# A graph layer on one core: edge products in rows of eight tiles, steps of 34 tiles, gathers without a per-gather wait

## What is computed

```python
h = relu(layernorm(x))
deg = max(segment_sum(1, dst), 1);  w = (deg[src] * deg[dst]) ** -0.5
edge_msg = relu(edge_attr @ W1e + b1e) @ W2e + b2e
agg = segment_sum((h[src] + edge_msg) * w, dst)
combined = (1 + gin_eps) * h + agg
out = h + relu(combined @ W1n + b1n) @ W2n + b2n
out = out * rsqrt(mean(out * out) + RMS_EPS) * rms_w
return x + out
```

## Time and profile before

| | |
|---|---|
| median device time of three runs | 1413.84 us |
| span of the profiled execution, first to last instruction | 1158.9 us |
| mean granted TensorE clock | 0.993 |
| busy TensorE, VectorE, ScalarE, GpSimd | 1061.3, 964.8, 734.5, 809.0 us |
| degree part (one-hot compares done to degrees ready) | 46.0 to 67.6 us |
| edge loop: first look, first products, last sum into the accumulator | 91.2, 103.5, 1106.5 us |
| gathers (L1008) | 784, mean 977 ns |

### The profile page before, as it was taken

The page is one execution under the profiler, slowest core; times in us unless marked ns, Lnnn a source line. Parts: engine busy times, 40 slices in busy tenths (PEclk is TensorE's granted clock), DMA queues, the critical chain, the costliest instruction groups (busy, mean ns, idle before and its releaser), DMA issues. The chain is left out here.

```text
span 1158.9 us, 35277 instructions
## 1 busy us (share of the span) xinstructions
PE 1061.3 (92%) x12293; PEld 764.4 (66%) x12293; DVE 964.8 (83%) x4508; ACT 734.5 (63%) x1317; POOL 809.0 (70%) x826
## 2 busy tenths in 40 slices
PE   0335999999999999999999999999999999999986
PEld 0322677777677777777777777777777777777753
DVE  7799988888888888888888888878888888888468
ACT  6953766666666666666666666666666666666535
POOL 1046777777777777777777777777777777777464
PEclk9999999999999999999999999999999999999988
DMA  6035444444444444444444444444444444443463
GB/s 221 1 142 156 133 118 120 129 118 120 130 119 118 129 120 118 129 120 119 128 120 119 128 119 119 130 118 120 128 118 120 129 118 120 130 119 80 129 255 119
DMA packets 67388, 145.56 MB, mean 126 GB/s; under 512 B 24163, under 2 KB 25750, under 8 KB 66832
## 3 DMA queue, kind: packets, MB, share of 16 engines
q1 hardware_dynamic: 41120, 88.27, 24.5%
q0 software_dynamic: 25088, 51.83, 18.8%
q10 hardware_dynamic: 1008, 3.21, 0.8%
HBM read 136.67 MB, written 6.57 MB: 124 GB/s over the span
## 5 line engine op out<-in xcount | busy, mean ns | idle before, releaser
L1008 POOL DMA_INDIRECT arena<-node_rows,idx x784 | 765.9, 977 | 247.7 <-issue 199.5
L1168 ACT ACTIVATE arena<-bank 128x686 f16<-128x686 f32 x414 | 375.9, 908 | 204.9 <-PE bank L1078 204.0
L1160 ACT ACTIVATE arena<-bank 128x512 f32<-128x512 f32 (+1 forms) x460 | 250.6, 555 | 157.3 <-PE bank L1033 141.0
L1089 PE MATMUL bank<-t_words,arena 128*126 128x256 f16 x2254 | 302.8, 275 | 0.4 <-ACT arena L1168 0.4
L1234 DVE SCALAR_TENSOR_TENSOR arena<-iota_h,hi_f,bank 128x98 f32<-128x98 f32 x828 | 226.1, 309 | 82.3 <-PE bank L1043 82.1
L1033 PE MATMUL bank<-w1e,arena 64*128 64x128 f32 x3312 | 253.9, 273 | 0.0
L1218 DVE TENSOR_SCALAR arena<-iota_c,code 128x343 f16<-128x343 f16 x828 | 241.6, 334 | 6.6 <-PE bank L1078 4.8
L1089 PEld LDWEIGHTS bank<-t_words,arena 128*126 128x126 f16 x2254 | 238.0, 136 | 1.7 <-ACT arena L1168 0.7
L1033 PEld LDWEIGHTS bank<-w1e,arena 64*128 64x128 f32 x3312 | 222.4, 191 | 0.0
L1078 PE MATMUL bank<-arena 128*128 128x343 f16 x828 | 190.6, 312 | 0.2
L1204 DVE TENSOR_SCALAR arena<-arena,part_f 128x256 f16<-128x256 uint8 x414 | 147.1, 355 | 0.8 <-DVE t_words L612 0.6
(11 more groups left out here) (199 smaller groups left out, 863.7 us busy)
## 6 DMA issues: line engine op xcount, KB each, us to landing
arena<-in_attr SPq DMA_DIRECT2D x138, 384.0 KB
arena<-low_src SPq DMA_DIRECT2D x48, 288.0 KB, 5.4
arena<-node_rows,idx POOLq DMA_INDIRECT x784
node_rows<-arena SPq DMA_DIRECT2D x1, 3160.5 KB, 8.9
arena<-in_x ACTq DMA_DIRECT2D x7, 448.0 KB, 10.9
arena<-in_x SPq DMA_DIRECT2D x6, 512.0 KB, 13.4
out<-arena SPq DMA_DIRECT2D x12, 224.0 KB
arena<-node_rows SPq DMA_DIRECT2D x4, 516.0 KB, 8.8
```

Of the source, the lines that this page charges most:

```text
L1008: nc.gpsimd.indirect_dma_start(out=edge_rows[:, u, j, 0:ROW], out_offset=None, in_=table, in_offset=bass.IndirectOffsetOnAxis(ap=idx[:, u, ...
L1089: mm = nc.tensor.matmul(x_sum[0:XC, 0:2 * D], strip[:, u, k, :], T16[:, k, :], start=k == 0, stop=k == NBLK - 1)
L1160: ins = nc.scalar.activation(out.rearrange("p (j o) d -> p o j d", o=2), of, ACT.Relu)
L1168: nc.scalar.activation(strip[:, u, :, 2 * p * W:2 * p * W + 2 * W].rearrange("p k (t w) -> p t k w", t=2), pair_bank[:, :].rearrange("p (t ...
```

## The change

A step takes 34 tiles, 18 dense and 16 gathered, so there are 48 steps; the last 20 hold 33 tiles. A step has five **phases** instead of nine rounds. A phase does the edge products of two units, that is of eight tiles (six in phase 2, four in phase 4), into a product buffer whose full width is used; the looks of four tiles; and two pairs of counts, one right behind the products and one behind the spread. The spread takes 8, 8, 16 and 17 blocks in phases 0 to 3. All four units of gathered sums of the step before stand at the end of phase 1, all five of dense sums at the end of phase 4. Row buffers of VectorE's one-hot matrices go from 3 to 4 (`RL`) and from 2 to 3 (`PB`). The gathers lose their wait per gather and keep the one for the sums. The attribute loads are cut 8, 7 and 2 pairs. The degree part compares half steps of 17 tiles, 96 of them.

```diff
-TD, TG = 18, 18
+TD, TG = 18, 16
 TS = TD + TG
-U = TS // 4
+LOOKS = [0, 2, 4, 6, 8, 9]
 UNITS_D = [(0, 4), (4, 4), (8, 4), (12, 4), (16, 2)]
-UNITS_G = [(0, 2), (2, 4), (6, 4), (10, 4), (14, 4)]
+UNITS_G = [(0, 4), (4, 4), (8, 4), (12, 4)]
 UD, UG = len(UNITS_D), len(UNITS_G)
+U = UD + UG
+PHASES = [(0, 1), (2, 3), (4, 5), (6, 7), (8,)]
+NPH = len(PHASES)
+SPREAD_AT = [0, 8, 16, 32, 49, 49]
 UL = TD // 2
-RL = 3
+RL = 4
+PB = 3
...
+ATTR_PAIRS = [0, 8, 15, 17]
+ATTR_PHASES = [0, 2, 4, 5]
...
+DT = TS // 2
+DC = DT * W
...
-                rel_t = rel.rearrange("p (j t) -> p j t", t=TD)
+                rel_t = rel.rearrange("p (j t) -> p j t", t=DT)
...
                     for j in fetched(c, i):
-                        if c > 0:
-                            pool.wait_ge(strip_ready if j % 2 else z_ps, (c - 1) * U + (j // 2 + 5))
                         nc.gpsimd.indirect_dma_start(
...
+            def edge_mlp(c, u, p):
+
+                if p in ATTR_PHASES:
+                    pe.wait_ge(attr_in[u][ATTR_PHASES.index(p)], (c - u) * 8 + 16)
+                if not (isinstance(c, int) and c * U + PHASES[p][0] < 1):
+                    pe.wait_ge(r_ready, c * U + PHASES[p][0])
+                pairs = pairs_of(p)
                 for odd in range(2):
                     rowsof = slice(odd * ED, odd * ED + ED)
-                    nc.tensor.matmul(z_bank[:, odd * 512:odd * 512 + 2 * D], ones_bf[rowsof, :],
-                                     bias_split[rowsof, 0, 0:2 * D], start=True, stop=False)
-                for j in range(2):
+                    nc.tensor.matmul(z_bank[:, odd * 512:odd * 512 + len(pairs) * D], ones_bf[rowsof, :],
+                                     bias_split[rowsof, 0, 0:len(pairs) * D], start=True, stop=False)
+                for j, pair in enumerate(pairs):
                     for odd in range(2):
                         rowsof = slice(odd * ED, odd * ED + ED)
                         at = odd * 512 + j * D
-                        mm = nc.tensor.matmul(z_bank[:, at:at + D], attr[rowsof, u, 2 * k + j, :], w1e[rowsof, :],
-                                              start=False, stop=j == 1)
+                        mm = nc.tensor.matmul(z_bank[:, at:at + D], attr[rowsof, u, pair, :], w1e[rowsof, :],
+                                              start=False, stop=j == len(pairs) - 1)
                 mm.then_inc(z_ps, 1)

-            def look(c, k):
-
-                pe.wait_ge(low_t_ready, c * UL + (k + 1))
-                if not (isinstance(c, int) and c * UL + k < 1):
-                    pe.wait_ge(s_ready, c * UL + k)
-                for j in range(2):
-                    mm = nc.tensor.matmul(look_ps[:, j * LK:(j + 1) * LK], low_t[:, k % RL, j, :], s_parts[:, :],
-                                          start=True, stop=True)
+            def look(c, p):
...
             def one(c, u):
-                for k in range(U):
+                for p in range(NPH):
+                    counts = range(2 * p, min(2 * p + 2, NA))
                     if live(c):
-                        edge_mlp(c, u, k)
+                        edge_mlp(c, u, p)
+                        count_pair(c, u, counts[0])
                     if live(c + 1):
-                        look(c + 1, k)
-                    if c == S and k == 0:
-                        for b in range(7):
-                            spread_rows(c - 1, 1 - u, b)
-                    elif c < S and live(c - 1) and 1 <= k < 8:
-                        spread_rows(c - 1, 1 - u, k - 1)
-                    if live(c):
-                        count_pair(c, u, k)
-                    if live(c - 2) and k == 2:
+                        look(c + 1, p)
+                    if live(c - 2) and p == 0:
                         window_gathered(c - 2)
                         window_dense(c - 2)
-                    if live(c - 1) and k < UG:
-                        sum_gathered(c - 1, 1 - u, k)
-                    if live(c - 1) and k == 6:
+                    if c == S and p == 0:
+                        spread_rows(c - 1, 1 - u, 0, NBLK)
+                    elif c < S and live(c - 1) and SPREAD_AT[p] < SPREAD_AT[p + 1]:
+                        spread_rows(c - 1, 1 - u, SPREAD_AT[p], SPREAD_AT[p + 1])
+                    if live(c) and len(counts) > 1:
+                        count_pair(c, u, counts[1])
+                    if live(c - 1) and p == 1:
+                        for i in range(UG):
+                            sum_gathered(c - 1, 1 - u, i)
+                    if live(c - 1) and p == NPH - 1:
                         turn(c - 1)
-                    if live(c) and k >= U - 4:
-                        sum_dense(c, k - (U - 4))
-                        if k == U - 1:
-                            sum_dense(c, UD - 1)
+                    if live(c) and p == NPH - 1:
+                        for k in range(UD):
+                            sum_dense(c, k)
             steps(pe, one)
...
             def one(c, u):
+                if live(c - 2):
+                    act.wait_ge(turned_ps, c - 1)
+                    if not (isinstance(c, int) and c < 3):
+                        act.wait_ge(win_d_ps, c - 2)
+                    nc.scalar.activation(turned, turned_bank, ACT.Copy).then_inc(turned_ready, 1)
                 if live(c - 1):
                     act.wait_ge(summed_d, c * UD)
                     if not (isinstance(c, int) and c < 2):
                         act.wait_ge(turned_ps, c - 1)
                     nc.scalar.activation(sum_d, sum_d_ps, ACT.Copy).then_inc(sum_d_ready, 1)
-                for k in range(U):
-                    if live(c - 1) and k == 5:
+                for p in range(NPH):
+                    if live(c - 1) and p == 2:
                         act.wait_ge(summed_g, c * UG)
                         if not (isinstance(c, int) and c < 2):
                             act.wait_ge(win_g_ps, c - 1)
                         nc.scalar.activation(sum_g, sum_g_ps, ACT.Copy).then_inc(sum_g_ready, 1)
-                    if live(c - 1) and k == 7:
-                        act.wait_ge(turned_ps, c)
-                        if not (isinstance(c, int) and c < 2):
-                            act.wait_ge(win_d_ps, c - 1)
-                        nc.scalar.activation(turned, turned_bank, ACT.Copy).then_inc(turned_ready, 1)
                     if live(c):
-                        relu(c, u, k)
-                        if k < NA:
+                        for k in PHASES[p]:
+                            relu(c, u, k)
                             keep_counts(c, u, k)
             steps(act, one)
...
+            def pairs_ahead(c, u, which):
+                if live(c):
+                    pair(c, u, which)
+
             def one(c, u):
+                for p in range(NPH):
+                    last = p == NPH - 1
+                    if c == S + 1 and p == 0:
                         nc.vector.tensor_scalar(rel_s[:, :, :], rel_s[:, :, :], float(-W), None, ALU.add)
                         step(nc.vector.tensor_scalar(rel_d[:, :, :], rel_d[:, :, :], float(-W), None, ALU.add))
+                    if c == -1 and p < 4:
+                        encode(nc, p, code, hi_f, rel_d, loop.scratch, step)
+                    if last:
+                        pairs_ahead(c + 1, 1 - u, 0)
+                    else:
+                        pairs_ahead(c, u, 2 * p + 2)
+                    if live(c + 1) and not last:
+                        for k in range(LOOKS[p + 1], LOOKS[p + 2]):
+                            turn_low(c + 1, 1 - u, k)
+                    if live(c + 2) and last:
+                        for k in range(LOOKS[0], LOOKS[1]):
+                            turn_low(c + 2, u, k)
+                    if live(c - 1) and p == 0:
+                        scale_gathered(c - 1, 1 - u, 2)
+                        scale_gathered(c - 1, 1 - u, 3)
+                    if live(c - 1) and last:
+                        keep_x(c - 1)
+                    if live(c) and p < 3:
+                        for j in range(2 * p, min(2 * p + 2, UD)):
+                            match_dense(c, j)
+                    if live(c - 2) and p == 1:
+                        add_windows(c - 2)
+                    if live(c - 1) and p == 2:
+                        places(c - 1)
+                    if live(c) and p in (2, 3):
+                        for j in (range(0, 3) if p == 2 else range(3, UD)):
+                            scale_dense(c, u, j)
                     if live(c + 1):
+                        for k in range(LOOKS[p], LOOKS[p + 1]):
+                            pick_s(c + 1, 1 - u, k)
+                    if live(c) and p in (2, 3):
+                        match_gathered(c, 2 * p - 4)
+                        match_gathered(c, 2 * p - 3)
+                    if last:
+                        pairs_ahead(c + 1, 1 - u, 1)
+                    elif 2 * p + 3 < NA:
```

(20 more changed lines are left out.)

145 lines of the change are left out of this document (54 added, 91 removed).

## The result

The changed kernel takes 1953.55 us (median of four runs, 1945.93 to 1956.55) against 1413.53 us: ratio 1.381, interval [1.377, 1.384]. The forecast was 1371, range 1356 to 1403. It was wrong by 583 us, and the change made the kernel slower instead of faster.

A forecast was written before the change was run, and what follows sets the result against it. TensorE was taken to set the step, with GpSimd full too. 47 steps of 19.7 us, 5 hold and 1 outside make 931.9 against 974.4, so 1413.84 - 42.5 = 1371 us, range 1356 to 1403.

The forecast's parts named there:

- the span and the median: Whole run: profiled span 1158.9 us, median of runs 1413.84; the 254.9 us between them were carried over unchanged.
- Taking the per-gather wait away saves no time at once, since it costs none: GpSimd's gathers: the 0.30 us before each is no wait, so removing the wait was priced at no saving.
- hold of 5 us: Edge loop: GpSimd's gathers let step 28 start only at about 657 us, where TensorE alone would be at 651.5.
- Rival A: Edge loop: GpSimd becomes the bound beside denser VectorE work, gather pitch 1.275 to 1.33 us; 1401 us, chance 0.18.
- C: Edge loop: TensorE and ScalarE alternate, 0.35 us lost in each of four phases, step 21.1 us; 1432 us, chance 0.08.
- D: TensorE's gaps are semaphore waits, not array changes, so the new order keeps them; step 20.9 us, 1423 us, chance 0.06.
- the 0.6 us of stalls: TensorE waits for ScalarE's copy at phase 1's second count, 0.2 us, and at phase 4's count, 0.4 us, each step.
- Step 19.7: Edge loop: a step falls from 21.65 us to 19.1 by TensorE's work, plus 0.6 of stalls, making 19.7 us.
- GpSimd full: Edge loop of the kernel before: 17 gathers at 1.275 us take 21.68 us, so GpSimd is full in step with TensorE.
- Prelude +1: Before and after the loop: 96 half-step columns instead of 92 cost 0.9 us; net +1, range -1 to +7.
- Compares at 1.02: Degree part: seven compares with rows of 17 bf16 instead of 18 stay at 1.02 us each; cost 0, possibly +6.5.

The follow-up runs named there:

- b1_same: The kernel before, unchanged, run again at the upper level to get a trace: 1438.23 us, beside 1435.44 for the kernel before.
- a2_after: The changed kernel, with nothing further changed, run again at the lower level: 1132.74 us against 1159.58 for the kernel before.

## Why the prediction was wrong

**The step that failed first: the span and the median.** The prediction found 254.9 us between span and median and carried them over. They do not lie there: b1_same has 1.7 us between span and run, the changed kernel's profiled execution 1.7 (1944.2 to 1945.93). They lie in the loop, 5.5 us in each of 46 steps, and the trace shown is of an execution without them. That was the sign to read: the page describes another level than the one that is timed, so the margins in the earlier trace rows could not be trusted for it.

**The step that failed worst: "Taking the per-gather wait away saves no time at once, since it costs none".** With it the sum put the loss by gathers at 0 beyond the hold of 5 us. True at the lower level, where the earlier trace rows were taken. At the upper level that wait was what kept the kernel before at 1435: without it 1784.04, and with such a wait the changed kernel takes 1616.46 instead of 1945.6. The wait is worth 329 to 349 us; the other 182 us of the changed kernel's loss stay open. The prediction asked what the wait costs, and what follows when GpSimd starts later, never what a wait holds back that starts too early. Rival A came nearest in place (GpSimd beside denser work) but had the direction wrong: GpSimd did not get slower (996 ns a gather at the lower level and 964 at the upper, 977 in the kernel before), it held the others up. C and D were about TensorE and ScalarE. (D's 20.9 us a step also leaves out the 0.6 us of stalls that the forecast has; with them it is 21.5.)

**The rest, held against a2_after at the lower level.** Span 1131.0 against 1158.9, -27.9, where the sum said -42.5 and the range -58 to -11.
- *Step 19.7*: 20.03. Four gathered sums in a row take 531.91 - 530.04 = 1.87 = 4 x 0.43 + 0.15, exactly as priced from the earlier trace rows, so D falls: the gaps were array changes. The rule that the prediction cites from the Trainium skill ("TensorEngine Tiling (Array Packing)", Key Properties), a drain for a change of mode and none for a change of tile, agrees with it. Four pairs take 1.21 (526.78 to 527.99; priced 1.23), the dense sums 1.22. What was mis-sized: a count directly behind products takes 0.33 to 0.34 (527.99 to 528.33), not 0.29, in four of the five phases, which is most of 0.2; and by the starts the two stalls are 0.26 (1.14 from 528.50 to 529.64, where phase 0 has 0.88 from 525.51 to 526.39) and 0.50 (1.16 from 519.45 to 520.61, where 0.66 was priced), not 0.2 and 0.4, together the rest. Over 47 steps the error is 15.7 us, which is the whole miss at this level (14.6 us); the other terms nearly cancel.
- *Hold 5 at step 28*: 3.7, in one step.
- *GpSimd full*: right as a reading at this level, but with little consequence; with a quarter of the gathers the times fall by 0.2 us before and 4 to 5 after.
- *Prelude +1*: step 1's first product starts at 122.40 instead of 119.58, +2.8; the end of the loop gives 1.8 back.
- *Compares at 1.02*: right.

```profile
L540 DVE TENSOR_SCALAR arena<-t_words x7: 1003/1006/1010, 39.5 to 45.0; 128x1632 bf16<-128x1632 f32 x7
```

Against 1019 in the earlier trace rows: 17 instead of 18 in the inner dimension costs nothing. The condition that the prediction cites from the Trainium skill ("VectorE: DVE Perf Modes", Mode 2×_2P), an even outermost dimension, holds for both, and these rows agree with it.

So the sum answers to the change at the lower level, with a third of the forecast gain lost to prices that were too low: the -27.9 us are inside the range that was forecast. The timed kernel is at the upper, where the loss is over 500 us and the term that the prediction set to zero is shown to be 329 to 349 of them.

## What to carry to other kernels

When the span of a trace and the timed median are a hundred us apart, find out which level the trace shows before pricing anything. A wait that costs nothing may still be doing work: it spreads what stands behind it, so before taking it out ask what a burst of that will do to everyone else. In both orders of this kernel indirect gathers tied to the pace of the engines that they hold up cost less than gathers in a burst, though pacing did not bring all of the loss back; a change to them is to be timed at both levels.

## What the runs showed of the hardware

- The same kernel has two levels, the same for all runs taken together: 1159 to 1160 or 1411 to 1438 for the kernel before, 1133 or 1946 to 1954 for the changed one, 1137 or 1616 with pacing. Runs on the same chip number stand at different levels, so what sets the level stays open.
- At the upper level a run of indirect gathers goes with late signals of TensorE, and of TensorE alone: ScalarE and VectorE resume together, 4.3 us after the start of a burst of 16, then mostly at 14.2 and at 22.9, some 3 us behind the last gather. In long bursts TensorE also stops where its program has no wait (94.1 us in the spread, 0.0 in bursts of four). Plain copies of the same size, on the same queue, twice as dense, do neither (one run). What inside GpSimd, TensorE or the signal path stalls is not shown.
- The time that the upper level adds, divided by the gathers, grows with the bunching: 0.32 to 0.36 us in the kernel before (254 to 279 us over 784; that gathers are its cause there is not tested), 0.45 in bursts of four (98 over 216), 0.64 paced by ReLU and copy (480 over 748), 1.10 in bursts of 16 (821 over 748). The last two contain the lower clock (0.896 and 0.804 on average).
- A plain copy of 128 rows occupies GpSimd for 0.55 us, an indirect one for 0.96 to 1.00 plus 0.30.
- No run has a wait for the landing of the gather two before, which would bound how many are under way; with one semaphore for four gathers its value does not tell which of them landed.
